# Attention rows normalised straight from PSUM with centred weights, and a last pass whose expert weights lie on chip and whose tiles use four PSUM banks

## The reference

```python
x = x + _L0_conv_ref(_gn(x), ...)         # group norm, depthwise conv, selective scan over 2304 tokens, gate, projection
t = _to_tokens(x)
t = t + _L1_attn_ref(_ln_t(t), ...)
t = t + _L1_ffn_ref(_ln_t(t), ...)

def _L1_attn_ref(x, norm_gamma, w_qkv, w_out, out_gamma):   # 8 heads of 16
    x = layer_norm(x, norm_gamma)
    q, k, v = jnp.split(jnp.einsum('bnc,fc->bnf', x, w_qkv), 3, axis=-1)
    q = jax.nn.softmax(q, axis=-1) * scale
    k = jax.nn.softmax(k, axis=-2)
    context = jnp.einsum('bhnd,bhne->bhde', k, v)
    out = jnp.einsum('bhde,bhnd->bhne', context, q)
    out = jnp.einsum('bnf,cf->bnc', out, w_out)
    return layer_norm(out, out_gamma)      # (out - mean) * rsqrt(var + 1e-5) * gamma

def _L1_ffn_ref(x, Wg, W1, W2, W3, b3):    # 8 experts, F = 384, the two best of each token
    C = weights of the top 2 of softmax(x @ Wg)
    act = silu(x @ W1[e]) * (x @ W3[e] + b3[e])
    out = sum over e of C[e] * (act @ W2[e])
```

## Time and profile before

| | |
|---|---|
| median of the runs | 3913.9 us |
| the profiled execution's own time | 3908.72 us |
| its span | 3906.9 us |
| granted TensorE clock, mean | 0.91 |
| busy: PE, DVE, ACT, POOL | 3163.4, 2983.4, 2553.7, 2909.4 us |
| pass 1 (attention joins), 444 to 815 us | 371 us |
| a full pass, the seventh, 2557.4 to 2995.1 us | 437.7 us |
| the pass without scan, from 3416 us to the end | 491 us |

### The profile page before, as it was taken

The page is one execution under the profiler, slowest core; times in us unless marked ns, Lnnn a source line. Parts: engine busy times, 40 slices in busy tenths (PEclk is TensorE's granted clock), DMA queues, the critical chain, the costliest instruction groups (busy, mean ns, idle before and its releaser), DMA issues.

```text
span 3906.9 us, 68984 instructions
## 1 busy us (share of the span) xinstructions
PE 3163.4 (81%) x17390; PEld 2012.8 (52%) x17390; DVE 2983.4 (76%) x5234; ACT 2553.7 (65%) x6158; POOL 2909.4 (74%) x3055
## 2 busy tenths in 40 slices
PE   5687888778889888988889887988889888776772
PEld 3233354335556555655556555655556555566662
DVE  3698989988898888878897788888898788822110
ACT  3455677457867777676867777676867777665451
POOL 1465757686769886888868897888968887966755
PEclk9788999789989998999989999999989999988896
DMA  3965656465869677886869677886869677856773
GB/s 89 221 146 129 157 124 162 120 161 137 221 177 263 153 211 197 222 221 163 233 178 244 158 208 194 231 212 162 231 185 260 157 202 195 235 150 182 241 233 109
DMA packets 420323, 730.02 MB, mean 187 GB/s; under 512 B 56203, under 2 KB 313814, under 8 KB 417750
## 3 DMA queue, kind: packets, MB, share of 16 engines
q1 hardware_dynamic: 302422, 484.13, 49.7%
q10 hardware_dynamic: 99072, 203.47, 17.0%
q0 software_dynamic: 18432, 37.93, 3.5%
HBM read 596.93 MB, written 100.07 MB: 178 GB/s over the span
## 4 chain that ended last, share of the span: by engine, by line
PE 24%; POOL 22%; issue 21%; DVE 15%; ACT 11%; DMA 4%; ACTq 2%; SPq 1%; POOLq 1%; DVEq 0%; PEldq 0%
POOL prod L698 10%; DVE state L1582 6%; PE ps_conv L901 5%; PE ps_main L967 4%; DVE ps_x L1569 3%; POOL got L821 3%; PE ps_g L1085 2%; DMA dt_rep<-dt_dram 2%; POOL rows_in L798 2%; PE ps_g L1092 2%; POOL hidden L810 2%; PE ps_y L981 2%; ACT dt_rep L1206 2%; PE ps_h L1073 2%; PE ps_x L915 1%
## 5 line engine op out<-in xcount | busy, mean ns | idle before, releaser
L698 POOL TENSOR_TENSOR prod<-state,c_rep 128x384 f32<-128x384 f32 x1536 | 1532.7, 1007 | 608.5 <-DVE state L1582 588.7
L1582 DVE TENSOR_TENSOR_SCAN state<-dt_rep,carry,ps_x 128x384 f32<-128x384 f32 x1280 | 1285.8, 1005 | 0.0
L1569 DVE TENSOR_TENSOR ps_x<-ps_x,db_rep 128x384 f32<-128x384 f32 x1536 | 852.9, 555 | 243.0 <-PE ps_x L915 223.7
L1206 ACT ACTIVATE dt_rep<-dt_rep,vecs 128x384 f32<-128x384 f32 x1536 | 917.8, 615 | 137.9 <-DMA dt_rep<-dt_dram 77.7
L915 PE MATMUL ps_x<-x_stack,copy 96*128 96x384 bf16 x1536 | 534.2, 350 | 310.8 <-DVE state L1582 306.4
L901 PE MATMUL ps_conv<-gx,w_conv 128*128 128x384 f32 x1728 | 689.6, 507 | 8.0 <-DVE parts L1599 4.6
L915 PEld LDWEIGHTS ps_x<-x_stack,copy 96*128 96x128 bf16 x1536 | 153.9, 100 | 681.6 <-DVE state L1582 493.1
L1390 ACT ACTIVATE g_sb<-ps_g,w_down 128x128 f32<-128x128 f32 x1032 | 304.2, 371 | 231.1 <-PE ps_g L1092 226.3
L901 PEld LDWEIGHTS ps_conv<-gx,w_conv 128*128 128x128 f32 x1728 | 301.1, 195 | 216.6 <-issue 129.6
L1073 PE MATMUL ps_h<-u_t,w_up 128*128 128x128 f32 x2064 | 327.5, 298 | 104.0 <-DVE silu L1799 80.0
L810 POOL TENSOR_TENSOR hidden<-g_sb,silu 128x384 f32<-128x384 f32 x344 | 343.7, 999 | 83.9 <-ACT u_out L1396 74.8
(11 more groups left out here) (256 smaller groups left out, 4958.7 us busy)
## 6 DMA issues: line engine op xcount, KB each, us to landing
dt_rep<-dt_dram SPq DMA_DIRECT2D x384, 768.0 KB
w_up<-in_w_exp ACTq DMA_DIRECT2D x344, 384.0 KB
w_down<-in_w_exp ACTq DMA_DIRECT2D x344, 193.5 KB
x_stack<-parts SPq DMA_DIRECT2D x576, 48.0 KB
u_in<-rows_in SPq DMA_DIRECT2D x344, 64.5 KB
rows_out<-u_out SPq DMA_DIRECT2D x344, 64.0 KB
dt_dram<-dt SPq DMA_DIRECT2D x192, 96.0 KB
qv<-in_x SPq DMA_DIRECT2D x48, 192.0 KB
```

The source lines that it names most:

```text
L698: pool.tensor_tensor(prod[:, k % HS, :], state[:, k % HS, :], c_rep[:, c % 2, :], ALU.mult).then_inc(s_prod.sem, 1)
L1206: act.activation(dt_rep[:, g % XS, q, :], dt_rep[:, g % XS, q, :], ACT.Exp, scale=decay_rate).then_inc(s_decay.sem, 1)
L1569: dve.tensor_tensor(x_n, x_n, db_rep[:, c % 2, :], ALU.mult).then_inc(s_inflow.sem, 1)
L1582: dve.tensor_tensor_scan(state[:, k % HS, :], dt_rep[:, g % XS, q, :], ps_x[k % XB][:, 0:T], init, ALU.mult, ALU.add).then_inc(s_state.sem, 1)
```

## The change

Five edits.

1. **Weights.** In setup DVE takes the mean of each row of `w_proj` away (`s_centre`), so that the attention's output has mean zero in every token; beside it lies a second copy times `out_gamma`. `ctx_o` has 256 columns.
2. **`ap` in place of `ao`.** Nine uses of two row tiles each (`T_AP`). PE makes plain and weighted rows (128 x 256 each). ACT squares the plain ones with a sum over the row, and makes the rate by a logarithm and an exponent. DVE multiplies the weighted rows in PSUM by the rate and adds the residual (`add_rows`), then takes the statistics. The first of the two normalisations, its statistics, L775 and L780 go.
3. **Places.** `acc` moves from q's buffer to `u_tok`, and x of the next image is loaded 16 steps earlier. Second normalisation, logits, routing, scatter and the last gathers move earlier; `AMONG` has 8 tiles at 88 to 122, the others run evenly from 128 to 220.
4. **Last pass, weights.** Decay, state, C and dB of the scan lie in one `arena`. When the last scan is over, SP loads the weights of all 8 experts into it. For `p` and `j` DVE copies 768 columns and ACT 387 columns of a tile's weights from there.
5. **Last pass, banks and engines.** For `p` and `j` odd tiles use `ps_x2` and `ps_y` beside `ps_h` and `ps_g`; DVE adds the bias and adds up the gathered rows. `p` begins at step 50, not 34; `T_END` becomes 407.

```diff
-T_TURN = (124, 129, 129, 131, 128, 130)
-T_XLOAD = 114
+T_TURN = (113, 115, 120, 120, 128, 130)
+T_XLOAD = 98
+T_QT, T_AP = (64, 66, 67, 71, 75, 79), (68, 69, 72, 73, 76, 77, 80, 81, 83)
-AMONG = (81, 84, 87, 90, 93, 96, 99, 102, 107, 112, 119, 126, 132)
-T_AMONG, T_LAST = 137, 220
+AMONG = (88, 91, 94, 98, 103, 110, 117, 122)
+T_AMONG, T_LAST = 128, 220
...
+        dt_rep, state = of_scan(XS, QD, T), of_scan(HS, T)
+        c_rep, db_rep = of_scan(2, T), of_scan(2, T)
...
+                    if ended.has_all_weights(m) and name[0] in "hg" and int(name[1:]) % 2:
+                        b = {HB: HB2, GB: GB2}[b]
...
+                for e in range(NE):
+                    sp.dma_start(every[:, e, :], a["w_exp"][e]).then_inc(s_every.sem, 16)
...
-                        pool.tensor_tensor(k_tok[:, tiles, :], k_tok[:, tiles, :],
-                                           out_gamma[:, :].unsqueeze(1).broadcast_to([P, TT, D]), ALU.mult).then_inc(s_gam.sem, 1)
-                        pool.tensor_tensor(acc[:, tiles, :], acc[:, tiles, :], k_tok[:, tiles, :], ALU.add).then_inc(s_acc.sem, 1)
...
+                    for k in range(2):
+                        r = P * (2 * g + k)
+                        ins = pe.matmul(o[:, 2 * D * k:2 * D * k + 2 * D], turned[:, r:r + P], ctx_o[:, :], start=True, stop=True)
...
+                    for k in range(2):
+                        t = 2 * g + k
+                        ins = act.activation(k_tok[:, t, :], aux(name, m)[:, 2 * D * k:2 * D * k + D], ACT.Square, accum_out=mv[:, t, 0:1])
+                    ins.then_inc(s_square.sem, 1)
+                    due(act, s_square, m, g + 1)
+                    act.activation(mv[:, tiles, 1], mv[:, tiles, 0], ACT.Ln, bias=eps_ln, scale=1.0 / D).then_inc(s_aln.sem, 1)
+                    due(act, s_aln, m, g + 1)
+                    act.activation(r2[:, tiles], mv[:, tiles, 1], ACT.Exp, scale=-0.5).then_inc(s_rms.sem, 1)
...
+            def tile_out(m, u):                       # ACT
+                v = u - LAG
+                if v >= 0:
+                    act.wait_ge(*full(m, f"g{u}"))
+                    if u < NU:
+                        due(act, s_plus, m, u + 1)
...
+                    act.activation(u_out[:, v % UOUT, :], aux(f"g{u}", m)[:, F:F + P], ACT.Copy,
+                                   scale=u_in[:, v % UIN, D:D + 1]).then_inc(frees(f"g{u}", m), 1)
+                if u + WA < NU:
+                    act.wait_ge(*full(m, f"g{u}"))
+                    copy_weights(m, u + WA)
...
+            def add_rows(m, a):                       # DVE
+                due(dve, s_rms, m, a + 1)
+                for k in range(2):
+                    t = 2 * a + k
+                    ins = dve.scalar_tensor_tensor(out=acc[:, t, :], in0=aux(name, m)[:, 2 * D * k + D:2 * D * k + 2 * D],
+                                                   scalar=r2[:, t:t + 1], in1=acc[:, t, :], op0=ALU.mult, op1=ALU.add)
...
+            def tile_plus(m, u):                      # DVE
+                dve.wait_ge(*full(m, name))
+                if u < NU:
+                    due(dve, s_down[u % WB], m, u // WB + 1)
+                    for k in range(MF):
+                        o = slice(P * k, P * k + P)
+                        ins = dve.tensor_scalar(g_sb[:, u % 2, o], aux(name, m)[:, o], w_down[:, u % WB, F + k:F + k + 1], None, ALU.add)
...
+                if u + WA < NU:
+                    copy_weights(m, u + WA)
```

More of the change, by code:

```diff
@@ L6 @@
+import math
 from contextlib import ExitStack
@@ L316, in image_of @@
             return i.j + i.ahead if isinstance(i, Next) else i
-        banks = [ps_main, ps_h, ps_g, ps_conv, ps_main, ps_x[0], ps_x[1]]
-        MAIN, HB, GB, CB, FB, XA, XB2 = range(7)
+        banks = [ps_main, ps_h, ps_g, ps_conv, ps_main, ps_x[0], ps_x[1], ps_x[2], ps_y]
+        MAIN, HB, GB, CB, FB, XA, XB2, HB2, GB2 = range(9)
         placed = [(f"z{hf}0", MAIN) for hf in range(HV)]
@@ L332, in build @@
         aux_of = {}
-        aux_per = [0] * 7
+        aux_per = [0] * len(banks)
         for name, b in placed:
@@ L473, in build, with weights_of @@
         assert min(b - a for a, b in zip(TILE, TILE[1:])) >= 2
+        def weights_of(e, first, last):
+            return every[:, bass.ds(e, 1), first:last].rearrange("p o f -> p (o f)")
         def image_rows(dram, i):
@@ L1451, in experts @@
                             act.sem_inc(s_sp.sem, 1)
-                        weights(m, u)
+                        if u == 0 and all_weights:
+                            act.wait_ge(s_every.sem, 16 * NE)
+                        if all_weights:
+                            copy_weights(m, u)
+                        else:
+                            weights(m, u)
                 for u in range(2):
```

278 lines of the change are left out of this document (167 added, 111 removed).

## The result

The changed kernel takes 4005 us (4000.6 to 4013.2) beside 3913.3 (3904.3 to 3920.4) of the kernel before on the same chip: ratio 1.024, 95% interval 1.021 to 1.027. I had forecast 3860. The profiled span is 4007.3 us, 100.4 more than before.

The account below looks back on a forecast made before the run. No engine limits a full pass throughout; the full one differs by stretch. Full passes -36, last pass -16, earlier turns in pass 0 -1: profiled 3908.7 becomes 3856, the median 5 higher, predicted 3860 us; range 3800 to 3905.

Parts of the forecast that it names:

- 144 to 192 and the first 28 steps of the next pass: Full-pass steps with evenly spaced tiles: 1.3 tiles more with PE full, +3 us a pass.
- Steps 88 to 112: Full-pass stretch: POOL falls from 51 to 38 and ACT from 52 to 44, -8 us, bounds 0 and -10.
- Steps 64 to 88: Full-pass stretch: POOL swaps products for gathers and sums, ACT rises to about 45 of 48 us; -1 us.
- Steps 112 to 128: Full-pass stretch: turns of next x, places and routing bring about 7 us of DVE; +4 us.
- 128 to 144: Full-pass stretch: DVE loses about 9 us, seven tiles for four bring PE to 43; -3 us, bounds 0 and -7.
- Last pass: Sum of the terms for the last pass, covering weights, cadence, attention, end, load and copies: -16 us.
- The end: After the last tile: 18 sums and their hops leave POOL, -14 us of 67, bounds -14 and -5.
- the attention: Last pass, attention of image j: POOL work and normalisations go, ACT work and table loads come; -4 us, bounds -20 and +10.
- The cadence: Last-pass tiles: ACT and DVE form a ring, 3.0 us a tile replacing 2.84; +5 and +4 us.
- The gain in the passes does not appear: Rival, 10%: PE is the true limit, full passes give 0 and the last pass some -10; 3903 us.
- DVE waiting for rates: Rival, 10%: in passes with scan DVE's row addition waits for ACT's exponent, 1.5 us a piece; 3955 us.
- DVE and POOL exclude each other: Rival, 12%: last-pass DVE copies and sums meeting POOL take 0.8 us more each; 3891 us.

Follow-up runs that it names:

- e_crowd: Changed kernel with tiles from step 137 on placed as in the kernel before and the five others at 125 to 134; 3926.5 us, ratio 1.003.
- e_two: Changed kernel with two tiles moved by one step, 138 to 137 and 140 to 139; 3978 us, ratio 1.018.
- e_oldsteps: e_all with everything behind the normalised rows at the steps of the kernel before; 3904 us, ratio 0.997.
- e_turn: Changed kernel with the next image's x load and turns at the steps of the kernel before; 3992 us, ratio 1.020.
- e_nolast: Changed kernel with last-pass weights from HBM, one bank each, bias on ACT and sums on POOL as before; 3997 us, ratio 1.021.
- e_load: Changed kernel with the eight experts' weights loaded one by one at steps 33 to 47, not all at step 27; 4002 us, ratio 1.024.
- e_all: Changed kernel with 13 tiles one by one then row from 137, old turns and x load, last-pass bias before silu, experts' weights loaded singly; 3914.3 us.

## Why the prediction was wrong

The profiled span is 100 us longer: 86 up to the last scan, where I had -37, and 15 in the last pass, where I had -16.

- **"144 to 192 and the first 28 steps of the next pass", "+3", was the step that failed.** Measured: +11 in steps 144 to 192 and +2 in 0 to 32, so +13. It priced the tiles by their number and PE's share. The number is right (one more), the places were not looked at: with the old places from 137 on, e_crowd is 9 and 5 us a pass shorter there, and 81 us in all. At steps 138 and 140 e_two shows how: a tile's table load and tanh delay an exponent, DVE waits for it with the silu behind, PE waits 5.09 us for `ps_h`, and its clock halves. Its row was in sight: the earlier trace rows show PE waiting for silu before `ps_h` at every tile. I took that for a fixed 0.27 us; in a full pass it is whatever DVE has in front of that silu. For most of steps 144 to 192 only the places are shown, not the meeting.
- **Steps 88 to 112, "-8": measured -2.2 (mean of four passes).** In the seventh pass ACT lost 5.6 us where I had 8 and POOL 5.7 where I had 13, and even so the stretch did not follow: the time went into waits. e_oldsteps, with the rows' relief at the old steps, has 55.2 for 56.7.
- **Steps 64 to 88, "-1": +1.5.** I had ACT rise "to about 45 of 48"; it has 35.6 of 50.2, and the full engine is DVE with 47.5. Of DVE I took "even, -2 to +2 us"; its busy time rose by 3.6 us (43.9 to 47.5) though three tiles left. One L1739 takes 340 ns, which is the row I had chosen, but I took a part of it for overlapped. The group in the seventh pass:

```profile
L1739 DVE SCALAR_TENSOR_TENSOR big_u<-ps_g,r,big_u 128x128 f32<-128x128 f32 x10 | 3.0, 341 | 0.0
L1398 ACT ACTIVATION_READ_ACCUMULATOR big_k<-ps_g 128x1 f32 x10 | 2.0, 203 | 0.0
```

- **Steps 112 to 128, "+4": +4.5, right.** DVE is the full engine there, 36 of 39.9 us, and e_turn shows that the turns are 3.8 of it. **128 to 144, "-3": -0.6**; with two tiles one step off, -5.6.
- **Last pass, "-16": +15.** The end, "-14": -13.7, right. The stretch up to the first scatter took 18 us more, where I had -4 for the attention and +2 for the load of the weights. It is 176 us in e_nolast, as before, so it comes with the weights on chip or what goes with them; one by one (e_load) 9 us of it are gone, and the other 9 are open. The cadence of 3.0 us was 3.18: right ring, mis-sized overlap. I took 0.5 us off for it; from start to start the trace shows 0.3, as the hand-overs from one engine to the other overlap next to nothing (tanh to silu 0.51 us for the 0.49 taken, bias to `u_out` 0.95 for 0.99). With the bias first the last image's tiles come every 2.4 us, and with the other three edits the last pass gains 45 us in place of my 16. That DVE's order was one link and free to choose, I hadn't seen.
- **The rivals.** "The gain in the passes does not appear" comes nearest, for another reason than I gave. Of DVE waiting for rates (3955) the trace shows 0.4 us in a pass. "DVE and POOL exclude each other" had the right mechanism and size (0.77 us more for a copy, I had 0.8), but the changed kernel hardly meets it: its copies are 2.2 us longer in sum, and of the 22 that overlap an indirect DMA of POOL three are longer, by 0.2 us. That was luck of the order; in e_all it is 22 us over the 86 copies.

## What to carry to other kernels

When work is moved on a fixed schedule, don't price it by stretch and engine share alone: at each new place, look at what stands on the freeing engine ahead of the instruction that frees the bank. Two constants moved by one step were worth some 25 us, all places together 80, more than any other edit here. Lay two kernels side by side step by step, and look at the granted clock behind each stall. Where work goes over to idle engines, add up the ring of hand-overs, and try the order of two independent operations in it before anything larger.
